# An audio tower on one Trainium2 core: W0 folded into the v weights, one ring of four PSUM buffers, rows by residue mod 3

## What is computed

```python
h = conv1d(sign(x), sign(kernel)) + bias            # x (4, 750, 128) -> (4, 748, 64)
h = (h - moving_mean) * rsqrt(moving_var + 1e-3) + beta
h = h + attention(layernorm(h));  h = h + tree_ffn(layernorm(h))

def attention(x):                                   # b, n, d, h = 4, 748, 64, 8
    qkv = x @ Wqkv + bqkv
    q, k, v = reshape(qkv, (3, b, n, d, h))         # flat: q is the first third of all values
    score = einsum('bnqh,btqh->bnth', q, k) * d ** -0.5
    attn = softmax(score, axis=1)
    av = einsum('bnnh,bnqh->bnqh', attn, v)         # only the diagonal of attn is used
    return av.reshape(b, n, d * h) @ W0 + b0

def tree_ffn(x):                                    # depth 7, 255 nodes
    # at each of 8 levels: score = x . w1[node] + b1[node]; out += gelu(|score|) * (x @ w2[node] + b2[node])
    # next node = 2 * node + 1 + (score > 0)
```

## Time and profile before

| | us |
|---|---|
| median of 3 runs | 549.22 |
| lowest, highest | 548.09, 549.48 |
| profiled execution, its own time | 548.32 |
| its span | 546.5 |
| VectorE busy, ScalarE busy, PE busy | 366.0, 299.8, 378.2 |
| GpSimd busy | 277.4 |
| mean granted TensorE clock | 0.892 |

### The profile page before, as it was taken

How to read it: one execution, slowest core, us unless ns; L and a number is a source line. 1 busy time by engine, 2 the same in 40 slices (tenths; PEclk the granted TensorE clock), 3 DMA queues, 4 the chain that set the end, 5 groups by cost and what they waited for, 6 DMA issues and landing times.

```text
span 546.5 us, 8746 instructions
## 1 busy us (share of the span) xinstructions
PE 378.2 (69%) x3014; PEld 251.9 (46%) x3014; DVE 366.0 (67%) x594; ACT 299.8 (55%) x655; POOL 277.4 (51%) x315
## 2 busy tenths in 40 slices
PE   1333859888898988988588993556109996587780
PEld 1222525444465645655355651554007774354450
DVE  0644495878867789687888788625956999443341
ACT  2463767999888998889588694002001110254440
POOL 1456594322236287362677506838375777741211
PEclk9999996999999999999799996655558999599996
DMA  5202497397330333302331300750014110200000
GB/s 130 65 1 54 114 229 150 86 196 131 86 86 14 73 86 86 86 22 65 85 85 34 86 1 4 129 84 4 16 35 109 40 43 22 73 9 5 7 5 7
DMA packets 52029, 36.03 MB, mean 66 GB/s; under 512 B 25122, under 2 KB 50687, under 8 KB 51980
## 3 DMA queue, kind: packets, MB, share of 16 engines
q1 hardware_dynamic: 48238, 32.47, 27.4%
q0 software_dynamic: 2944, 2.45, 1.7%
q10 hardware_dynamic: 800, 0.49, 0.4%
HBM read 10.57 MB, written 8.79 MB: 35 GB/s over the span
## 4 chain that ended last, share of the span: by engine, by line
ACT 29%; PE 26%; DVE 25%; issue 8%; POOL 6%; DMA 3%; ACTq 0%; SPq 0%; POOLq 0%; DVEq 0%
ACT S L943 15%; PE S L735 5%; DVE nm L1097 5%; PE U L674 5%; DVE lm L1268 4%; DVE vT L1261 3%; ACT q L930 3%; ACT vT L930 3%; PE S L838 3%; ACT k L930 3%; DMA par<-in_L_tok_moving_var 2%; PE U L838 2%; POOL pool_a L459 2%; PE S L840 1%; POOL w L452 1%
## 5 line engine op out<-in xcount | busy, mean ns | idle before, releaser
L1097 DVE TENSOR_REDUCE nm<-S 128x1 f32<-128x748 f32 x192 | 171.9, 932 | 44.7 <-PE S L735 41.9
L943 ACT ACTIVATE S<-S,nm 128x748 f32<-128x748 f32 x192 | 167.1, 885 | 42.6 <-DVE nm L1097 41.4
L735 PE MATMUL S<-pool_a 128*128 128x512 f16 (+1 forms) x768 | 151.6, 332 | 29.6 <-ACT S L943 27.1
L735 PEld LDWEIGHTS S<-pool_a 128*128 128x128 f16 x768 | 68.9, 105 | 91.7 <-ACT S L943 56.2
L550 POOL DMA_INDIRECT out<-lm,vT x44 | 43.4, 985 | 58.1 <-DVE lm L1274 51.1
L459 POOL TENSOR_TENSOR pool_a<-q,pool_a 128x750 f16<-128x750 f32 x16 | 25.8, 1613 | 72.3 <-DVE pool_a L1064 72.1
L635 PE MATMUL U<-xhT,wq 128*128 128x250 f16 x288 | 42.9, 289 | 17.7 <-ACT q L930 8.2
L1268 DVE TENSOR_REDUCE lm<-vT 128x64 f32<-128x512 f32 x44 | 45.1, 1026 | 1.6 <-DVE vT L1261 0.5
L943 ACT ACTIVATION_READ_ACCUMULATOR S<-S,nm 128x1 f32 x192 | 44.0, 229 | 0.0
L635 PEld LDWEIGHTS U<-xhT,wq 128*128 128x128 f16 x288 | 27.1, 104 | 35.5 <-ACT q L930 13.7
L491 POOL DMA_INDIRECT sorted_rows<-xrow,slot x24 | 26.9, 1119 | 18.4 <-DVE slot L1183 10.3
(11 more groups left out here) (214 smaller groups left out, 681.6 us busy)
## 6 DMA issues: line engine op xcount, KB each, us to landing
pool_a<-pool_a SPq DMA_DIRECT2D x64, 187.5 KB, 3.0
pool_a<-pool_a SPq DMA_DIRECT2D x64, 93.8 KB, 2.8
sorted_rows<-zrow SPq DMA_DIRECT2D x1, 3864.0 KB, 22.3
vT<-sorted_rows SPq DMA_DIRECT2D x11, 276.0 KB, 3.7
w<-in_L_ffn_w2s SPq DMA_DIRECT2D x1, 2048.0 KB
lm<-in_x SPq DMA_DIRECT2D x4, 375.0 KB
pool_a<-in_L_ffn_w2s SPq DMA_DIRECT2D x1, 1024.0 KB
out<-lm,vT POOLq DMA_INDIRECT x44, 2.1
```

What stands on the lines that cost most here:

```text
L735: last = mm(S[n % 3][:, c0:c1], kst[:, u % 3, a, hd, START[t]:START[t] + P], qst[:, u % 3, hd, c0:c1], start=(a == 0), stop=(a == 1))
L943: sc_.activation(S[n % 3][:, 0:N], S[n % 3][:, 0:N], ACT.Exp, bias=nm[:, b % 2, j, i:i + 1], accum_out=sm[:, b % 2, j, i:i + 1]).then_inc( ...
L1097: v.tensor_reduce(nm[:, b % 2, j, i:i + 1], S[n % 3][:, 0:N], X, ALU.max, negate=True).then_inc(s_max, 1)
```

## The change

1. **W0 goes into the v weights.** Attention's output for a token is the sum over heads of its factor times (v row of the head) @ (W0 rows of the head). The kernel now makes, in units 0 and 1, the product of the v weights with W0 (`v_weights_T`, `v_times_w0`, split into high and low parts by ScalarE and VectorE) and that of the v bias (`v_bias_w0`, kept as rows `cb`). For each unit, `heads_out` multiplies the normalised tokens with these (18 matmuls of 128 columns), so that a token's row for both heads of the pair stands in PSUM. VectorE multiplies it with the factors (`weigh_heads`, 768 columns), GpSimd adds both heads to h (`add_heads`, two additions of 384 columns). The v projection, its drain, `broadcast`, the product with v and `out_proj` are gone. The factors are finished once a unit (`diag_shift`, `diag_exp`, `diag_weights`), not once a batch.
2. **One ring.** Four buffers Z0 to Z3 take all results of PE in the order in which PE makes them. `order` lists them, `fills(u, i)` says which come behind step i of unit u, and `take` makes PE wait until the result four places earlier was freed, by ScalarE (`by_act`) or VectorE (`by_dve`). The diagonal has a turn of its own, all six tiles at once.
3. **Rows by residue mod 3.** q and k are kept as three blocks of rows with the same residue, tiles have 125 rows instead of 128, drains write contiguously. Since h comes out of the convolution in token order, it goes to a DRAM tensor `h_rows` (9 DMAs) and comes back in the new order (24 DMAs of up to 125 rows of 256 bytes). The DMAs are issued by SP after the stacks of units 2, 3 and 4. GpSimd adds b0 when they are back (`h_bias`), in unit 2.
4. **Layer norm groups.** The first layer norm works on four groups of tiles instead of four batches. Group 0 holds the first tiles of batches 0 and 1, all that the first four projections need. They are made behind group 0. Group 1 and the convolution of group 2 stand ahead of the first score on PE, centering and normalising of group 2 ahead of the first maximum on VectorE. The rest of groups 2 and 3 is placed in units 0 and 1.
5. In the tail, the sums of the second layer norm, ranks of batch 2, transposes and logits of batch 3 follow each other in the ring. The loads of x for batches 2 and 3 now stand behind the parameters.

```diff
-        def projections(u):
-            if u == 0:
-                return {1: ("v", 0, 0), 3: ("v", 1, 0), 5: ("q", 2, 0), 7: ("k", 2, 0), 9: ("v", 2, 0)}
-            if u + AHEAD < NU:
-                return {1: ("q", u + AHEAD, 0), 3: ("k", u + AHEAD, 0), 5: ("v", u + AHEAD, 0)}
+        FIRST = [("q", 0), ("k", 0), ("q", 1), ("k", 1), ("xb", 2), ("xb", 3), ("xh", 1), ("cv", 2)]
+        def fills(u, i):
+            b, ph = u // NPAIR - 1, u % NPAIR
+            f = []
+            if 1 <= u <= NU and i == 0:
+                f.append(("d", u - 1))
+            if u + AHEAD < NU and i in (1, 3):
+                f.append(("qk"[i // 2], u + AHEAD))
+            f += {(0, 4): [("xh", 2)], (0, 5): [("cv", 3)], (0, 7): [("wt", 0)], (0, 9): [("wm", 0)],
+                  (0, 11): [("wt", 1)], (1, 2): [("wm", 1)], (1, 4): [("xh", 3)], (1, 5): [("wt", 2)],
+                  (1, 7): [("wm", 2)], (1, 9): [("cb", 0)], (1, 11): [("w1", 0)], (2, 5): [("y", 0)],
+                  (2, 9): [("y", 1)]}.get((u, i), [])
+            if 3 <= u <= NU and i == 5:
+                f.append(("y", u - 1))
+            if b >= 0 and ph == 2:
+                f += {5: [("t", b)], 8: [("l", b, 0)], 10: [("l", b, 1)]}.get(i, [])
+            if b >= 1 and (ph == 3 if b < B - 1 else ph == 1) and i == 7:
+                f.append(("r", b - 1))
...
+            def take(f):
+                if number[f] >= 4:
+                    pe.wait_ge(*freed[order[number[f] - 4]])
+                return zone(f)
...
+                for t in range(NT):
+                    r0, g = v_tile(b, t)
+                    zt = z[0:XP, t * P:(t + 1) * P]
+                    for a in range(2):
+                        mm(zt, xhT[:, r0:r0 + XP], mw[:, a, g * H * D + j * P:g * H * D + (j + 1) * P],
+                           start=(a == 0), stop=False)
+                    last = mm(zt, pick[:, g, 0:XP], cb[:, js], start=False, stop=True)
...
+            def weigh_heads(w):
+                dve.wait_ge(s_at, w + 1)
+                dve.wait_ge(*full(("y", w)))
+                if w >= 2:
+                    dve.wait_ge(s_hy, w - 1)
+                av = at[0:XP, w % 4].rearrange("p (a t) -> p t a", a=2).unsqueeze(3).to_broadcast([XP, NT, 2, D])
+                v.tensor_tensor(prod[0:XP, w % 2], zone(("y", w))[0:XP, 0:NT * P].rearrange(
+                    "p (t a o) -> p t a o", t=NT, a=2), av, ALU.mult).then_inc(s_wyv, 1)
...
+                if u == 2:
+                    h_bias(0)
+                    h_bias(1)
+                    h_bias(2)
+                    h_bias(3)
+                    add_heads(0)
+                    add_heads(1)
+                if 3 <= u < NU:
+                    add_heads(u - 1)
```

More of the change, by code:

```diff
@@ L26 @@
 DUP = NT * P - N
+CLASSES = (1, 2, 0)
+CLASS_N = {0: 250, 1: 249, 2: 249}
+CLASS_AT = {1: 0, 2: 249, 0: 498}
+HALF = 125
+KST = [CLASS_AT[c] + HALF * h for c in CLASSES for h in range(2)]
+TOKEN0 = [3 * HALF * h + c for c in CLASSES for h in range(2)]
 TT = B * NT
@@ L637, in project @@
-                if w >= 1:
-                    n = 2 * "qkv".index(kind)
-                    last = diagonal(w - 1, range(n, n + 2))
-                last.then_inc(s_uf, 1)
-            def diagonal(w, tiles):
+                        for e0, e1 in cuts:
+                            last = mm(z[:, e0:e1], wq[:, a, g * H * D + j * P:g * H * D + (j + 1) * P],
+                                      xhT[:, r0 + e0 - at0:r0 + e1 - at0], start=(a == 0), stop=(a == 1))
+                last.then_inc(s_full, 1)
@@ L644, in diagonal @@
+            def diagonal(w):
+                z = take(("d", w))
                 pe.wait_ge(s_prod, w + 1)
-                for t in tiles:
-                    last = mm(U[:, U_D + t:U_D + t + NT + 1:NT], qk[:, START[t]:START[t] + P], sel[:],
+                for t in range(NT):
+                    last = mm(z[0:XP, t:t + NT + 1:NT], qk[:, w % 3, KST[t]:KST[t] + XP], sel[:],
                               start=True, stop=True)
-                return last
-            def broadcast(b, j):
-                if j == 0:
-                    pe.wait_ge(s_at, b + 1)
-                if b == B - 1 and j >= 1:
-                    pe.wait_ge(s_ue, unit_no[("bc", b, j)] - 1)
-                else:
-                    fill(("bc", b, j))
+                last.then_inc(s_full, 1)
@@ new lines, in v_bias_w0, with heads_out @@
+            def v_bias_w0():
+                z = take(("cb", 0))
+                pe.wait_ge(s_bq, 32)
+                for h in range(H):
+                    last = mm(z[0:3, h * D:(h + 1) * D], bqn[0:D, :, h], w0n[:, h, :], start=True, stop=True)
+                last.then_inc(s_full, 1)
+            def heads_out(w):
+                b, j = divmod(w, NPAIR)
+                z = take(("y", w))
+                if w == 0:
+                    pe.wait_ge(*freed["wm", 2])
+                    pe.wait_ge(s_cb, 1)
+                    pe.wait_ge(s_id, 2)
+                pe.wait_ge(*xhat_ready(GROUPS_FOR["v"][b]))
+                js = slice(j * P, (j + 1) * P)
@@ L750, in _ @@
                         scores(u, i)
[L751 to L759 removed]
+                    for f in fills(u, i):
+                        fill(f)
             pe.wait_ge(s_m7, B)
[L762 removed]
+            pe.wait_ge(*freed["r", B - 1])
+            U = Z[3]
             mm(U[:, 0:1], run[:, NT, :], ones[:, 0:1], start=True, stop=True).then_inc(s_cnt, 1)
@@ L977, in _ @@
+            take(("xh", 1))
+            x_hi(2)
             for u in range(NU + NPAIR):
```

908 lines of the change are left out of this document (505 added, 403 removed).

## The result

The changed kernel takes 582.36 us (median of 4 runs, 578.66 to 583.75) against 548.88: 1.060 times the kernel before, with a 95% interval of 1.0545 to 1.0656. Measured again beside other runs it was 1.0565 (1.0547 to 1.0583). The prediction said 527. The profiled execution took 581.13 us, its span is 579.4.

A forecast was written before the change was run, and what follows sets the result against it. The prediction took ScalarE to set the loop, between a start and a tail. Start -7.5, loop -4.5 and tail -10.5 sum to -22.5: 525.8 us for the profiled execution, 527 for the median, range 503 to 543.

The forecast's parts named there:

- A plain unit of the loop: Loop units without batch work: 12.8 us of ScalarE work plus 2.2 lost around y, 15.1 with small waits, +0.35 each.
- The buffer rule: In the loop's ring, a result takes its buffer only when the fourth before is free; y waits for exponential 3, losing 1.2 us.
- The other units: Loop units after a batch: units one and two save 17.5 us over three batches; unit three rises from 16.42 to 18.4.
- Unit 14: Late loop unit: VectorE waits some 3 us more for GpSimd's squares, as slots and head sums put GpSimd behind.
- Rival 2: Units 0 to 3: moved centering, normalising, W0 results and GpSimd's lateness cost 10 us more, 537 us; chance 0.20 shared with Rival 4.
- The start: Up to the first exponential: it comes at 53.4 us instead of 60.85, -7.5 us, bounds -12 and -3.
- Rival 4: Start: unit 0's scores still wait for all groups, so it gains nothing, 534 us; chance 0.20 shared with Rival 2.
- The tail: Last exponential to path masks: GpSimd decides, 30.5 us instead of 41.0, -10.5 us, bounds -13 and -6.
- GpSimd's lock: Unit 1: VectorE's subtraction meets GpSimd's memset of w7 and is charged nothing; if locked, 4 us more.
- h through DRAM: 33 new DMAs on SP's queue: nothing charged, head additions done at 116.9, weighing in unit 3 at 119.2, 2 us to spare.
- rival 3: Row DMAs take 2.24 us each instead of 0.61, so VectorE stands at weighing: up to 563 us; chance 0.12.
- rival 1: Loop: the ring hides y, so 1.7 to 2.2 us in thirteen units go, -22, 505 us; chance 0.15.

The follow-up runs named there:

- experiment 8: The kernel with 128-row bias tiles, with GpSimd's slot scatters of batches 0 and 1 moved later: 0.977 of the kernel before, 535.89 us.
- Experiments 1 and 5: The run listed as experiment 1 and the padded kernel, each with its own line here.
- experiment 2: The changed kernel with 128 instead of 125 weight columns in all eighteen y matmuls: 1.030 of the kernel before.
- padded kernel: The changed kernel with the two bias tiles of y zero-padded from 35 to 128 rows: 1.008 of the kernel before, 552.85 us.
- all edits together: The changed kernel with y at 128 rows and columns, two W0 products and group 2's centering early, GpSimd's scatters later: 0.965 of the kernel before, 529.19 us.
- experiment 1: The changed kernel without the six 35-row matmuls that add the v bias in each y fill: 0.987 of the kernel before.

## Why the prediction was wrong, point by point

The change is 5.6 to 6% slower where 4% faster was forecast. Against the forecast's 525.8 for the profiled execution, the 581.1 measured are made of: start -1.0, units 0 and 1 +7.6, the lengthened y of units 2 to 13 and 15 +34.7 (their 260.1 us in after against 225.4 in experiment 8), other causes in these units +10.5, unit 14 +0.1, tail +2.4, last part +1.1. The 34.7 is more than the 27 us that padding gave the whole kernel, since with the short y unit 14 became some 8 us longer (27.2 against 19.1).

- **The failed step** is in *A plain unit of the loop*: "18 matmuls of 128 columns, at 1.49/24 each, 1.1 us". The row it came from the earlier trace rows has twenty-four matmuls of one shape, with 128 rows and 64 columns of weights. The six of y that add the bias have 35 rows of weights, and I took the row's price over to a mixed sequence. It was 2.73 us. Experiments 1 and 5 show the price right for one shape (0.74 for twelve, 1.09 for eighteen), experiment 2 shows the change of rows as the larger part. The Trainium skill has the rule (TensorEngine Tiling (Array Packing), § Key Properties): changing the tiling mode drains TensorE. The runs agree with it, at 0.10 us for each change with 128 columns and 0.14 with 125; that 35 rows are such a mode is my reading, not shown apart.
- **How 1.6 us a fill became 35.** The buffer rule was read rightly: PE stands at y until exponential 3 ends, and ScalarE has two exponentials in hand. So each 1.68 us of the longer fill (step 5 3.90 against 2.22) reached ScalarE in full: 14 fills, some 23 us. The other 11 stand in units 3, 5, 8, 10, 11 and 13, where the granted clock was lower. I had named a falling clock only as a sign, with no price; it fell.
- **The wait behind weighing**, 1.0: 0.97. **A plain unit**: 15.1 forecast, 17.36 measured, 15.68 with padded tiles. The 0.6 left is step 0 (2.39, 0.33 more than a drain and an exponential), step 2 (2.24) and step 5. "d, q and k fit" was too close: the diagonal now makes its twelve matmuls in one piece of 1.47 us ahead of the second score, and ScalarE waits 0.33 us for q.
- **The other units.** Units one and two after a batch came down once y was short (15.7, 16.1 and 18.2; 15.7 each), unit three 19.0 against 18.4. Not foreseen: the first step behind logits or ranks, 3.19 in units 7 and 11 and 4.85 in unit 12.
- **Unit 14**: 19.1, forecast 19.0, but this was luck. The forecast had 3 us more of waiting for GpSimd's squares; in the trace of after VectorE sums them without a wait, and in the padded kernel it waits 4.81 us (after, then the padded kernel):

```profile
342.10 0.54 DVE L1338 TENSOR_REDUCE ln<-sq 128x6 f32<-128x384 f32 x1
```
```profile
323.45 0.55 DVE L1338 TENSOR_REDUCE ln<-sq 128x6 f32<-128x384 f32 x1 [4.81 <-POOL sq L578]
```

  (The second profile of the changed kernel has 2.26 us.) With y as short as the forecast had it, unit 14 takes 27.2 us, 8 more than forecast: the wait for GpSimd was seen and sized too small, and the slow loop hid it. That GpSimd caught up because the loop was slower is my reading; no run shows it apart.
- **Units 0 and 1**: 47.6 against 40.0. I had sized ScalarE's work and VectorE's centering, and gave the float32 products no length of their own: 3.67 and twice 2.00 us of PE. Rival 2 had this mechanism, with 10 us.
- **The start**: 52.37, forecast 53.4. Right, by its own steps (first projection 27.4, forecast 28.4; convolution done 44.8, forecast 45.4; group 2 normalised 51.5, forecast 52.4). Rival 4 is wrong with it.
- **The tail**: 32.9, forecast 30.5. GpSimd's scatters end 20.0 us after the last exponential, not 17.1. Of this 1.8 us is that its masks begin 7.4 us before the end of the last exponential instead of 9.2, and 1.0 that masks and scatters take 27.4 us instead of 26.4. VectorE's two head sums beside them take 2.05 and 1.71 us where 0.56 is usual; each ends about 0.4 us after the GpSimd operation that ran when it began (the first at 386.01, GpSimd's at 385.59):

```profile
382.18 3.41 POOL L313 TENSOR_TENSOR ML<-lm 128x1530 f32<-128x1530 f32 x1
...
383.96 2.05 DVE L1294 TENSOR_TENSOR xrow<-xrow,va 125x384 f32<-125x384 f32 x1
```

  The comparison is locked for 4.21 us until the memset ends, as priced.
- **GpSimd's lock**: the subtraction in unit 1 took 0.67 us under the memset of w7, which ran from 95.46 to 102.38. Nothing to charge was right.
- **h through DRAM**, rival 3: the DMAs and GpSimd's additions of b0 in the kernel after:

```profile
L366 SPq DMA_DIRECT2D xrow<-h_rows x24: 273/350/648, 71.4 to 116.9; - x24
...
119.83 0.93 POOL L527 TENSOR_TENSOR xrow<-xrow,b0r 125x384 f32<-125x384 f32 x1 [1.62 <-DMA xrow<-h_rows]
```

  A row DMA holds SP for 0.35 us (median), not 2.24. The head sums behind the bias additions end at 124.7, 24.7 us into unit 2, where the forecast had 23.5 (116.9 less 93.4). Weighing in unit 3 comes at 131.41, so the cover held, with 6.7 us to spare where the forecast had 2. Rival 3 is wrong, and so is rival 1: y was never hidden.
- **The rivals and the range.** The range (503 to 543) rested on bounds for waits, collisions and DMAs, and on none for the length of a fill. The bound was to be had: a price taken from one shape of matmul for a sequence of two needed an upper end, and at 0.15 us each the same working (1.6 us more in 14 fills) gives some 22 us more than the 527: no gain, though not yet the loss that came. With the fill mended the kernel takes 552.85 us, still not faster than before, 26 us above the forecast: units 0 and 1, unit 14, the tail and 0.6 us a plain unit are left. Padding and GpSimd's new order together give 535.89, about half of the forecast's gain; only all edits together (529.19) come near the 527.

## What to carry to other kernels

Keep the number of weight rows the same through a sequence of short matmuls: pad a small operand with zero rows rather than let a narrow matmul stand between full ones; here that was worth 27 us for two lines. Where results share buffers in order, a fill's length goes straight into the waiting engine's time once less work is in hand than the fill takes, so price each fill by its own shape, with a lower and an upper bound. And after a change moves work to an engine that had room for it (GpSimd here), look at which of its queued operations someone waits for, and put the ones that nobody waits for behind it: that gave another 17 us.

## What the runs showed of the hardware

- Twelve matmuls of 128 x 125 weights and 128 columns pass at 0.062 us each although each of their weight loads shows 132 to 139 ns (experiment 1); with 35-row weights between, a group of three takes 0.46 us (0.38 with 128 columns) instead of 0.18.
- With the 35-row matmuls in y the granted clock of units 5 and 8 was 0.83 and 0.76 in the mean, with padded tiles 1.00. In unit 5 PE was busier by the profile at the lower clock (17.4 of 19.4 us) than at the full one (12.6 of 15.7): a high busy share is no sign of a high clock.
- The same code ran its units 0 and 1 in 54.6 us (padded kernel) and 48.0 us (experiment 8, where nothing ahead of unit 12 differs): the product at unit 1's third step took 3.67 us in one profile and 2.00 in the other. Why the clock differed there stays open.
- One set of runs had everything behind the loop some 20 us longer for every kernel profiled in it. Ratios within a set held; times across sets would have misled. The cause stays open.
